# Row maxima, silu and residual rows kept in PSUM, the first stage's calls reordered, and base units moved ahead of the first gathered rows

## The chip, the cores and the metric

One core of a Trainium2 chip runs the whole kernel. The metric is the device time of one execution in microseconds (us); the number quoted is the median of the runs. Below, PE is TensorE, DVE is VectorE, ACT is ScalarE, POOL is GpSimd and SP is SyncE, which here only issues DMAs.

## The reference: what is computed

Two gated sublayers on x of 4 x 256 x 256 (four sequences b, 1024 tokens in eight tiles of 128):

```
q(t, w): s = sqrt(max|t| / max|w|) per column; t/s and w*s are rounded to int8 steps by row;
         the product of the rounded values times both row scales        # smooth-quantised linear
h   = q(layernorm(x), fside);  a = silu(h[:, :128]) * h[:, 128:]
x   = x + tanh(g_xattn) * q(a, ctx)
n   = layernorm(x)
bids = sigmoid(n @ conf_W.T + conf_b) * wealth;  two best of 8 experts, softmax over the two
expert e: g = n @ base_gate + n @ gate_A[e] @ gate_B[e] / 4;  u likewise with up
          y = silu(g) * u;  out_e = y @ base_down + y @ down_A[e] @ down_B[e] / 4
x   = x + tanh(g_ffn) * sum of the two chosen out_e by their weights
```

## The kernel before, in words

**First stage.** For each b the quantised block runs as a chain of short calls, each a Python function with b as its argument: `stats`, `rstd_of`, `x_norm` (layernorm), `w_T`, `x_T1` (transposes), `w_max`, `x_max`, `quotient`, `roots` (column factors), `factors` (PE spreads them along rows), `smooth` (DVE multiplies and takes row maxima), `scale` (ACT rounds), `q1_T`, `q1T_out`, `row_w`, `w_row`, `products1`, `deq1`, `silu1`, `act_up`; then the same for the second product (`a_T`, `a_max`, `roots2`, `factors2`, `smooth2`, `scale2`, `q2_T`, `q2T_out`, `row_c`, `c_row`, `products2`), and the new residual and its layernorm (`x1_rows`, `rstd2_of`, `x1_norm`, `x2_T`, `x2_hi`, `x2_lo`). `logits(b)` gives the routing scores. Every engine executes its calls in a fixed order written out by hand; semaphores between engines do the rest, so a call that has to wait holds up all that stand behind it on its engine.

**Weights.** The second sublayer works in split precision (each weight as a high and a low part, three matmuls per product: lines 55, 57 and 59). 41 chunks of weights go through a ring `raw` of four buffers: SP loads chunk n (line 379) once the low part of chunk n-4 is made, ACT casts the high part (`split`, line 561), POOL subtracts for the low part (`lo`, line 425). Chunks 0 to 7 are the base weights, 8 to 11 the A factors (CH_A is 12), 12 to 27 the B factors, 28 to 36 the down factors (CH_1 is 37), 37 to 40 base_down.

**Base units.** `unit(u)` on PE makes a quarter of the gate and up base products of token tile u//4 (six matmuls of 448 columns, into bank 0 or 4), `unit_out(u)` on ACT copies it out (line 632) and every second one stores it to memory (`base_products`). There are 32. With PRE = 6 tiles, units 0 to 23 come before the plan and 24 to 31 after the first gathered rows.

**Plan and tiles.** After `logits(3)` DVE picks the two experts, PE ranks the pairs (lines 1459 to 1463), DVE works out their places, PE sorts (line 1471), DVE writes the token list (`tok`, line 1091, semaphore `s_plan`). POOL then gathers the normed rows of the first two tiles (`gather`), PE transposes them (`x_T`, line 1488), and 19 tiles of 128 pairs follow: `project_A`, `expand_B`, silu and product, `h_T` (line 1525), `down_products`, scatter. The first tile computes its base products directly (`base_product`, 24 matmuls in pG and pU); the later ones gather them (`gather_base`). On the first tile POOL also makes the low parts of chunks 37 to 40.

Of the kernel before, what the change touches and what calls it, by code (L numbers as in the profile page):

```python
# [23 lines left out]
ALU = mybir.AluOpType  # L24
# [8 lines left out]
P = 128  # L33
EPS = 1e-6
# [30 lines left out]
def build(nc, x, fside, ctxw, g_xattn, g_ffn, wealth, conf_W, conf_b,  # L65
# [22 lines left out]
    with stack:  # L88
# [38 lines left out]
        with part1:  # L127
# [10 lines left out]
            am1 = s1("am1", [P, NB, 4])  # L138
# [7 lines left out]
            am2 = s1("am2", [P, NB, 4])  # L146
# [135 lines left out]
        s_conf = sem("s_conf")  # L282
# [109 lines left out]
        def _(pool):  # L392
# [68 lines left out]
            lo(4)  # L461
            rstd_of(2)
            lo(1)
            roots(0)
            roots(1)
            lo(1)
            rstd_of(3)
            lo(6)
            roots(2)
            lo(1)  # L470
            roots(3)
            lo(6)
            roots2(0)
            lo(3)
            roots2(1)
            lo(2)
            rstd2_of(0)
            roots2(2)
            lo(3)
            rstd2_of(1)  # L480
            lo(5)
            roots2(3)
            lo(4)
            rstd2_of(2)
            lo(1)
            rstd2_of(3)

# [32 lines left out]
            for n in range(CH_1, NCH):  # L520
                split_lo(n)
# [14 lines left out]
        def _(act):  # L536
# [35 lines left out]
            a.activation(warm[:, :], expo[:, 1:2], ACT.Silu).then_inc(s_warm, 1)  # L572
            act.wait_ge(s_rounder, 2)
# [68 lines left out]
            split(12)  # L642
            scale(0)
            split(1)
            scale(1)
            q1T_out(0)
            split(1)
            q1T_out(1)
            w_row(0)
            split(2)  # L650
            silu1(0)
            w_row(1)
            split(4)
            scale(2)
            silu1(1)
            split(2)
            q1T_out(2)
            scale(3)
            scale2(0)
            w_row(2)  # L660
            q1T_out(3)
            q2T_out(0)
            silu1(2)
            split(1)
            w_row(3)
            c_row(0)
            scale2(1)
            split(2)
            q2T_out(1)
            split(2)  # L670
            c_row(1)
            silu1(3)
            split(2)
            x2_hi(0)
            split(2)
            scale2(2)
            split(2)
            q2T_out(2)
            split(1)
            x2_hi(1)  # L680
            split(1)
            unit_out(0)
            c_row(2)
            split(2)
            unit_out(1)
            unit_out(2)
            scale2(3)
            unit_out(3)
            unit_out(4)
            q2T_out(3)  # L690
            x2_hi(2)
            unit_out(5)
            c_row(3)
            unit_out(6)
            unit_out(7)
            unit_out(8)
            x2_hi(3)
            unit_out(9)
            unit_out(10)
            unit_out(11)  # L700
            a.activation(warm[:, :], expo[:, 1:2], ACT.Sigmoid).then_inc(s_warm, 1)
# [3 lines left out]
            for u in range(13, 20):  # L705
                unit_out(u)
# [3 lines left out]
            for u in range(20, 4 * PRE):  # L710
                unit_out(u)
# [66 lines left out]
            for t in range(PRE, NT):  # L778
                base_out(t)
# [27 lines left out]
        def _(dve):  # L807
# [53 lines left out]
            def smooth(b):  # L861
# [11 lines left out]
                link(v.tensor_scalar(sc1[:, b, :], am1[:, b, :], EPS, 1.0 / QMAX, ALU.max, ALU.mult))  # L873
# [29 lines left out]
            def smooth2(b):  # L903
# [5 lines left out]
                link(v.tensor_reduce(am2[:, b, :], q2[:, b], AX_X, ALU.max, apply_absolute_value=True))  # L909
                link(v.tensor_scalar(sc2[:, b, :], am2[:, b, :], EPS, 1.0 / QMAX, ALU.max, ALU.mult))  # L910
                v.reciprocal(inv2[:, b, :], sc2[:, b, :]).then_inc(s_inv2, 1)

            def x1_rows(b):

                dve.wait_ge(s_mm2, b + 1)
                dve.wait_ge(s_a, NB - 1)
                dve.wait_ge(s_crow, b + 1)
                for j in range(TB):
                    ins = v.scalar_tensor_tensor(out=hq[:, 0, j, :], in0=A[b][:, j * H:(j + 1) * H],
# [3 lines left out]
                xv_ = xs_all[:, 2 * b:2 * b + 2, :]  # L923
# [716 lines left out]
```

## Time and profile before

| | |
|---|---|
| median of 3 runs (lowest to highest) | 334.29 us (334.28 to 334.85) |
| the profiled execution, whole | 334.16 us |
| its span, first to last instruction | 332.40 us |
| PE busy / DVE / ACT / POOL | 264.7 / 201.7 / 159.1 / 128.0 us |
| mean granted TensorE clock | 0.90 of full |
| moved by DMA | 45.69 MB, 137 GB/s over the span |

Times inside the span are counted from its start. A row of a timeline gives start, duration, engine, line, operation, output and inputs with shapes and how many instructions it merges; in brackets stands how long the engine was idle before it and what ended that. PE durations overlap, so PE's cost is read from start to start.

### The profile page before, as it was taken

The page shows a single profiled execution, that of the slowest core. Times are in us where ns is not written, and L with a number is a line of the kernel's source. Part 1 is how long each engine was busy: PE and PEld are TensorE (multiplying, and loading weights), DVE is VectorE, ACT ScalarE, POOL GpSimd, SP SyncE. Part 2 cuts the span into 40 slices and gives each one's busy share as a digit, 9 for nine tenths or more (in the row PEclk, how much of TensorE's full clock was granted, in tenths as well). Part 3 has the DMA queues.
Part 4 walks back from the last instruction along what each step waited for, and adds up shares of the span by engine and source line. Part 5 has one row for each costly group of instructions (what it writes and reads, how often), then busy time and mean ns, then how long its engine had stood idle before and what let it go on. Part 6 is the DMA issues. An engine that isn't in the chain of part 4 may idle for free.

```text
span 332.4 us, 5189 instructions
## 1 busy us (share of the span) xinstructions
PE 264.7 (80%) x1556; PEld 241.5 (73%) x1557; DVE 201.7 (61%) x407; ACT 159.1 (48%) x283; POOL 128.0 (39%) x149
## 2 busy tenths in 40 slices
PE   0743947478998959949999999999999999997700
PEld 0532835377986849849999999999999999996600
DVE  1579697968316800166776767676767776775125
ACT  0634979575534413434555555555555555554011
POOL 4489782988000020092333333333333333311111
PEclk9977769659999969987999999999999999999855
DMA  6846351487434422261444444443343444400065
GB/s 192 245 134 169 96 166 55 115 202 236 159 145 166 164 91 110 110 221 34 142 144 134 139 140 142 142 142 134 135 142 142 142 142 142 142 16 18 16 218 176
DMA packets 31342, 45.69 MB, mean 137 GB/s; under 512 B 14104, under 2 KB 25760, under 8 KB 31328
## 3 DMA queue, kind: packets, MB, share of 16 engines
q0 software_dynamic: 4416, 21.50, 19.3%
q1 hardware_dynamic: 20752, 14.03, 14.7%
q10 hardware_dynamic: 6160, 9.98, 8.2%
q8 instruction: 8, 0.13, 0.2%
q14 instruction: 6, 0.05, 0.0%
HBM read 33.57 MB, written 11.93 MB: 137 GB/s over the span
## 4 chain that ended last, share of the span: by engine, by line
PE 64%; DVE 11%; DMA 9%; ACT 6%; POOL 5%; issue 3%; ACTq 1%; SPq 1%; DVEq 0%; POOLq 0%
PE pY L55 8%; PE pY L59 8%; PE pY L57 8%; PE pT L1525 5%; PE pG L55 3%; DMA q<-in_fside_BxS2xS_dram 3%; PE bank L55 3%; PE bank L57 3%; PE bank L59 3%; PE pG L57 3%; PE pG L59 3%; PE pU L57 3%; PE pU L55 3%; PE pU L59 3%; DMA yr<-results 2%
## 5 line engine op out<-in xcount | busy, mean ns | idle before, releaser
L507 POOL DMA_INDIRECT results<-yb,dest x19 | 18.8, 988 | 93.5 <-DVE yb L1173 93.5
L55 PE MATMUL pY<-Wd_hi,hT_hi 128*128 128x384 f32 x133 | 48.3, 363 | 1.0 <-ACT Wd_lo L743 0.8
L59 PE MATMUL pY<-Wd_hi,hT_lo 128*128 128x384 f32 x133 | 45.2, 340 | 0.0
L57 PE MATMUL pY<-Wd_lo,hT_hi 128*128 128x384 f32 x133 | 45.2, 340 | 0.0
L493 POOL DMA_INDIRECT xin<-normed,tok x19 | 18.6, 981 | 38.3 <-DVE share L1093 25.1
L501 POOL DMA_INDIRECT bin<-base_products,tok x18 | 22.0, 1220 | 27.6 <-PE pU L59 17.8
L632 ACT COPY brow<-bank 128x448 f32<-128x448 f32 x32 | 17.0, 532 | 25.6 <-PE bank L59 25.4
L753 ACT CAST hT_hi<-pT 128x896 fp32r<-128x896 f32 x19 | 17.2, 908 | 24.1 <-PE pT L1525 24.1
L729 ACT CAST xaT_hi<-pX 128x256 fp32r<-128x256 f32 x19 | 7.1, 374 | 42.4 <-PE pX L1502 42.0
L55 PEld LDWEIGHTS pY<-Wd_hi,hT_hi 128*128 128x128 f32 x133 | 25.5, 192 | 2.3 <-DVE hT_lo L1161 1.5
L55 PE MATMUL bank<-Wbase_hi,x2T_hi 128*128 128x448 f32 x64 | 25.7, 401 | 0.5 <-ACT brow L632 0.5
L57 PEld LDWEIGHTS pY<-Wd_lo,hT_hi 128*128 128x128 f32 x133 | 25.6, 193 | 0.0
L59 PEld LDWEIGHTS pY<-Wd_hi,hT_lo 128*128 128x128 f32 x133 | 25.4, 191 | 0.0
L57 PE MATMUL bank<-Wbase_lo,x2T_hi 128*128 128x448 f32 x64 | 24.6, 384 | 0.0
L59 PE MATMUL bank<-Wbase_hi,x2T_lo 128*128 128x448 f32 x64 | 24.5, 382 | 0.0
L1157 DVE TENSOR_TENSOR hbuf<-hbuf,gb 128x896 f32<-128x896 f32 x19 | 22.6, 1191 | 1.9
L1161 DVE TENSOR_TENSOR hT_lo<-pT,hT_hi 128x896 fp32r<-128x896 f32 x19 | 20.6, 1082 | 2.8 <-ACT hT_hi L753 2.8
L1130 DVE TENSOR_TENSOR xaT_lo<-pX,xaT_hi 128x256 fp32r<-128x256 f32 x19 | 8.1, 424 | 22.7 <-ACT xaT_hi L729 22.7
L1525 PE MATMUL pT<-ident,hbuf 128*128 128x128 f32 x133 | 18.4, 280 | 4.2 <-DVE hbuf L1157 4.2
L1167 DVE TENSOR_TENSOR zT_lo<-pX,zT_hi 128x128 fp32r<-128x128 f32 x19 | 5.5, 292 | 26.1 <-ACT zT_hi L760 26.1
L747 ACT ACTIVATE gb<-gb 128x896 f32<-128x896 f32 x19 | 18.1, 955 | 5.6 <-DVE gb L1144 5.4
L425 POOL TENSOR_TENSOR WB_lo<-raw,WB_hi 128x448 fp32r<-128x448 f32 x16 | 18.5, 1177 | 5.2 <-ACT WB_hi L561 5.2
(235 smaller groups left out, 739.5 us busy)
## 6 DMA issues: line engine op xcount, KB each, us to landing
base_products<-brow ACTq DMA_DIRECT2D x16, 448.0 KB, 2.5
yr<-results SPq DMA_DIRECT2D x8, 256.0 KB, 4.7
raw<-in_L_ffn_gate_B_dram SPq DMA_DIRECT2D x8, 224.0 KB, 2.6
raw<-in_L_ffn_up_B_dram SPq DMA_DIRECT2D x8, 224.0 KB, 2.6
raw<-in_L_ffn_down_A_dram SPq DMA_DIRECT2D x7, 256.0 KB, 3.0
x_resid<-in_x_dram SPq DMA_DIRECT2D x4, 256.0 KB, 5.2
q<-in_fside_BxS2xS_dram ACTq DMA_DIRECT2D x4, 256.0 KB, 8.0
normed<-q ACTq DMA_DIRECT2D x4, 256.0 KB, 2.7
```

What stands on the lines that cost most here:

```text
L55: m.matmul(outs[i], hi, whi[i], start=first, stop=False, skip_group_check=True)
L57: m.matmul(outs[i], hi, wlo[i], start=False, stop=False, skip_group_check=True)
L59: ins = m.matmul(outs[i], lo, whi[i], start=False, stop=last, skip_group_check=True)
L425: g.tensor_tensor(lo, src, hi, ALU.subtract).then_inc(s_wlo, 1)
L493: g.indirect_dma_start(out=xin[:, :], out_offset=None, in_=xn, in_offset=bass.IndirectOffsetOnAxis(ap=tok[:, j:j + 1], axis=0)).then_inc(d ...
L501: g.indirect_dma_start(out=bin_[:, j % 2].rearrange("p a i -> p (a i)"), out_offset=None, in_=gun, in_offset=bass.IndirectOffsetOnAxis(ap= ...
L507: g.indirect_dma_start(out=yg, out_offset=bass.IndirectOffsetOnAxis(ap=dest[:, j:j + 1], axis=0), in_=yb[:, :], in_offset=None).then_inc(d ...
L747: a.activation(gb[:, :], gb[:, :], ACT.Silu).then_inc(s_silu, 1)
L753: a.copy(hT_hi[:, :, :].rearrange("p c q -> p (c q)"), pT[:, :, :].rearrange("p a q -> p (a q)")[:, 0:I]).then_inc(s_hhi, 1)
L1157: v.tensor_tensor(hbuf[:, :], hbuf[:, :], gb[:, :], ALU.mult).then_inc(s_h, 1)
L1161: v.tensor_tensor(hT_lo[:, :, :].rearrange("p c q -> p (c q)"), pT[:, :, :].rearrange("p a q -> p (a q)")[:, 0:I], hT_hi[:, :, :].rearrang ...
L1525: ins = m.transpose(pT[:, c // 4, (c % 4) * P:(c % 4 + 1) * P], hbuf[:, c * P:(c + 1) * P], ident[:, :])
```

## The change

Row maxima: `smooth` and `smooth2` write them into the first four columns of bank A[b], whose factors have been used by then (both `smooth` multiplies are awaited first), in place of `am1` and `am2` in SBUF. `silu1` writes into bank A[4 + b] and `act_up` reads it there. `x1_rows` makes the new residual in bank A[b]; `bn_stats` and `x1_norm` read it there, and a new ACT call `resid(b)` copies it to `x_resid`; units (bank 0) and logits (bank 1) wait for that copy. SP waits for all of x before the first weight chunk; ACT issues its loads of conf_W, ctx, conf_b and wealth after its two table loads. The sigmoid's table is loaded right after `silu1(3)`. Units up to 29 come before the first gathered rows, 30 and 31 after them, and the direct base products of up and gate stand on either side of `xa_T(0)`. The low parts of chunks 37 to 40 move from POOL to DVE (`late_lo`, semaphore `s_wlo2`).

```diff
 sync:
+            for b in range(NB):
+                sp.wait_ge(d_x[b], 16)
-                    sp.wait_ge(s_wlo, n - RING + 1)
+                    sp.wait_ge(s_wlo, min(n - RING + 1, CH_1))
 gpsimd, after gather_base(2):
-            for n in range(CH_1, NCH):
-                split_lo(n)
 scalar:
-                a.activation(hq[:, b % 2, :, 0:I2], hq[:, b % 2, :, 0:I2], ACT.Silu).then_inc(s_sg, 1)
+                a.activation(A[4 + b][:, 0:2 * I2].rearrange("p (j q) -> p j q", j=TB), hq[:, b % 2, :, 0:I2], ACT.Silu).then_inc(s_sg, 1)
+            def resid(b):
+                act.wait_ge(s_x2, TB * (b + 1))
+                a.copy(xs_all[:, TB * b:TB * (b + 1), :].rearrange("p t h -> p (t h)"), A[b][:, :]).then_inc(s_resid, 1)
...
             x_hi(0)
-            for t in range(PRE, NT):
-                base_out(t)
+            unit_out(4 * NT - 2)
+            unit_out(4 * NT - 1)
 vector, smooth:
-                    dve.wait_ge(s_smooth, 2 * b + w + 1)
-                    v.tensor_reduce(am1[:, b, 2 * w:2 * w + 2], q1[:, b, 2 * w:2 * w + 2, :], AX_X, ALU.max,
+                    dve.wait_ge(s_smooth, 2 * b + 2)
+                    v.tensor_reduce(A[b][:, 2 * w:2 * w + 2], q1[:, b, 2 * w:2 * w + 2, :], AX_X, ALU.max,
 x1_rows:
-                dve.wait_ge(s_a, NB - 1)
-                    ins = v.scalar_tensor_tensor(out=hq[:, 0, j, :], in0=A[b][:, j * H:(j + 1) * H],
+                    ins = v.scalar_tensor_tensor(out=A[b][:, j * H:(j + 1) * H], in0=A[b][:, j * H:(j + 1) * H],
-                xv_ = xs_all[:, 2 * b:2 * b + 2, :]
-                v.tensor_tensor(xv_, xv_, hq[:, 0], ALU.add).then_inc(s_x1, 1)
+                xv_ = A[b][:, :].rearrange("p (t h) -> p t h", t=TB)
+                v.tensor_tensor(xv_, xv_, xs_all[:, 2 * b:2 * b + 2, :], ALU.add).then_inc(s_x1, 1)
...
+            def late_lo(n):
+                _, hi, lo, width = chunks[n]
+                dve.wait_ge(s_whi, n + 1)
+                v.tensor_tensor(lo, raw[:, n % RING, 0:width].rearrange("p (c h) -> p c h", h=H), hi, ALU.subtract).then_inc(s_wlo2, 1)
+            dve.wait_ge(s_resid, NB)
             x_lo(0)
...
             u_add(0, 0, True)
+            late_lo(CH_1)
+            late_lo(CH_1 + 1)
             xa_lo(1)
             h_mul(0)
+            late_lo(CH_1 + 2)
+            late_lo(CH_1 + 3)
 tensor:
-                pe.wait_ge(s_deq2, max(b + 1, 2))
+                pe.wait_ge(s_resid, 2)
...
             x_T(0)
-            base(PRE)
+            unit(4 * NT - 2)
+            unit(4 * NT - 1)
             pe.wait_ge(s_wlo, CH_A)
             project_A(0, group(0))
-            base(PRE + 1)
+            for c in range(HC):
+                base_product(1, c, xT_hi[:, c, :], xT_lo[:, c, :], False)
             xa_T(0)
             pe.wait_ge(s_copied, 4 * NT)
-            for gu in range(2):
-                for c in range(HC):
-                    ins = base_product(gu, c, xT_hi[:, c, :], xT_lo[:, c, :], False)
+            for c in range(HC):
+                ins = base_product(0, c, xT_hi[:, c, :], xT_lo[:, c, :], False)
```

The new orders of the calls, of POOL, ACT, DVE and PE (s, l, u, o stand for `split`, `lo`, `unit`, `unit_out`; 3s is three of them):

```
POOL rstd_of 0 1 2, 2l, rstd_of 3, l, roots 0 1 2, 7l, roots 3, 2l, roots2 0, 2l, roots2 1, l, roots2 2, 3l,
     rstd2_of 0, 2l, rstd2_of 1, l, roots2 3, 2l, rstd2_of 2, 8l, rstd2_of 3, 6l
ACT  8s, scale 0, 2s, scale 1, q1T_out 0, scale 2, w_row 0, q1T_out 1, silu1 0, s, q1T_out 2, w_row 1, s, scale 3,
     silu1 1, w_row 2, 2s, silu1 2, q1T_out 3, s, scale2 0, w_row 3, s, q2T_out 0, 2s, c_row 0, scale2 1, scale2 2,
     q2T_out 1, s, q2T_out 2, c_row 1, silu1 3, sigmoid table, s, resid 0, x2_hi 0, 2s, c_row 2, 2s, o0, s, o1, s, o2,
     s, o3, scale2 3, o4, resid 1, o5, x2_hi 1, q2T_out 3, x2_hi 2, resid 2, o6, 2s, c_row 3, 4s, o7, s, o8, s, o9,
     resid 3, o10, x2_hi 3, s, o11, s, o12, sigmoid, o13 to o20, shares, o21 to o29
DVE  stats 0 1 2, x_norm 0, w_max 0, x_norm 1, w_max 1, x_norm 2, x_max 0, w_max 2, stats 3, x_max 1, c_max 0, w_max 3,
     quotient 0 1, cW_out, x_max 2, quotient 2, c_max 1, x_norm 3, smooth 0 1 2, x_max 3, quotient 3, c_max 2 3, deq1 0,
     smooth 3, act_up 0, deq1 1, a_max 0, act_up 1, deq1 2, smooth2 0, a_max 1, act_up 2, a_max 2, smooth2 1 2,
     x1_rows 0, deq1 3, x1_norm 0, x1_rows 1, act_up 3, x2_lo 0, a_max 3, x1_rows 2, smooth2 3, x1_norm 1 2, x2_lo 1 2,
     x1_rows 3, x1_norm 3, x2_lo 3
PE   ... factors 0 1 2, x_T1 3, q1_T 0 1, row_w 0, products1 0, factors 3, q1_T 2, row_w 1, products1 1, row_w 2,
     products1 2, a_T 0, q1_T 3, factors2 0, a_T 1, row_w 3, products1 3, a_T 2, factors2 1, q2_T 0, factors2 2, row_c 0,
     products2 0, q2_T 1 2, row_c 1, products2 1, row_c 2, products2 2, x2_T 0, a_T 3, u0, u1, factors2 3, u2 to u4,
     x2_T 1 2, u5, q2_T 3, logits 0, u6, logits 1, row_c 3, products2 3, logits 2, u7 to u10, x2_T 3, u11, u12, logits 3,
     u13 to u17, rank, u18 to u23, sort, u24 to u29
```

## Rows read from the trace of the kernel before

**Rows 1.** Busy time by stretch: stretch, length, busy us per engine, clock, DMA

```profile
60.00:73.50 13.50, 7.61 (x36) 6.83 (x37) 11.03 (x21) 7.69 (x17) 12.30 (x13) 0.54 0.70 169
97.10:116.10 19.00, 17.39 (x124) 15.21 (x125) 12.28 (x53) 7.94 (x17) 0.00 (x0) 1.00 0.36 145
121.10:134.90 13.80, 13.40 (x59) 11.98 (x59) 0.85 (x2) 4.64 (x9) 0.96 (x1) 0.82 0.29 111
147.80:303.10 155.30, 155.13 (x959) 146.79 (x960) 107.43 (x174) 79.67 (x123) 53.90 (x51) 0.98 0.37 124
```

**Rows 2.** Timeline of PE between unit 0 and the first tile

```profile
73.52 0.72 PE L55 MATMUL bank<-Wbase_hi,x2T_hi 128*128 128x448 f32 x1
...
97.07 0.45 PE L55 MATMUL bank<-Wbase_hi,x2T_hi 128*128 128x448 f32 x1
...
105.36 0.20 PE L1459 MATMUL bank<-pickb,beforeb 128*128 128x64 bf16 x1 [1.15 <-DVE pickb L1035]
...
106.18 0.45 PE L55 MATMUL bank<-Wbase_hi,x2T_hi 128*128 128x448 f32 x1
...
113.65 0.74 PE L1471 MATMUL bank<-attrib,atrow 128*128 128x76 bf16 x16
...
121.07 0.66 PE L1488 MATMUL pX<-ident,xin 128*128 128x128 f32 x2 [4.13 <-DMA xin<-normed,tok]
...
128.46 0.28 PE L55 MATMUL pX<-WA_hi,xT_hi 128*128 x1
...
139.84 0.38 PE L1488 MATMUL pX<-ident,xin 128*128 128x128 f32 x2
...
147.79 1.75 PE L1525 MATMUL pT<-ident,hbuf 128*128 128x128 f32 x7 [4.16 <-DVE hbuf L1157]
```

**Rows 3.** Timeline of ACT: first rounding, and the sigmoid's table load

```profile
31.52 2.08 ACT L578 ACTIVATE q<-q,rounder,inv 128x256 f32<-128x256 f32 x4
...
99.51 1.28 ACT L701 ACT_TABLE_LOAD   x1 [0.39 <-ACT brow L632]
```

**Rows 4.** The chain that ended last: start, duration, what

```profile
27.68 3.30 DMA raw<-in_L_ffn_up_A_dram
...
117.15 3.78 DMA xin<-normed,tok
```

**Rows 5.** Timeline of DVE in the first stage and the plan

```profile
24.66 1.29 DVE L867 TENSOR_TENSOR q<-q,bank 128x512 f32<-128x512 f32 x2 [1.23 <-PE bank L1268]
...
39.16 0.88 DVE L882 SCALAR_TENSOR_TENSOR hq<-bank,sc,rowb 128x256 f32<-128x256 f32 x2 [2.25 <-ACT rowb L593]
...
53.47 0.88 DVE L882 SCALAR_TENSOR_TENSOR hq<-bank,sc,rowb 128x256 f32<-128x256 f32 x2 [0.72 <-ACT rowb L593]
...
76.54 0.88 DVE L919 SCALAR_TENSOR_TENSOR hq<-bank,sc,rowb 128x256 f32<-128x256 f32 x2 [0.91 <-ACT rowb L599]
...
88.25 0.88 DVE L919 SCALAR_TENSOR_TENSOR hq<-bank,sc,rowb 128x256 f32<-128x256 f32 x2 [0.83 <-ACT rowb L599]
...
101.61 0.23 DVE L1021 TENSOR_TENSOR bids<-bids,rows 128x64 f32<-128x64 f32 x1 [4.14 <-ACT bids L704]
...
115.92 0.18 DVE L1091 TENSOR_SCALAR tok<-dest 128x19 int32<-128x19 int32 x1
```

**Rows 6.** Tile hbuf: ns min/median/max, first to last start

```profile
L1157 DVE TENSOR_TENSOR hbuf<-hbuf,gb x19: 1092/1093/2949, 144.8 to 301.1; 128x896 f32<-128x896 f32 x19
```

**Rows 7.** Groups of ACT up to 140 us, by form

```profile
L621 ACT CAST x2T_hi<-bank 128x512 fp32r<-128x512 f32 x4 | 2.3, 583 | 1.3 <-PE bank L1338 1.0 <-issue 0.3
```

**Rows 8.** Groups of POOL up to 150 us, by form: busy us, mean ns, idle before

```profile
L425 POOL TENSOR_TENSOR WB_lo<-raw,WB_hi 128x448 fp32r<-128x448 f32 x16 | 18.5, 1177 | 5.2 <-ACT WB_hi L561 5.2
```

**Rows 9.** Groups of DVE up to 100 us, by form

```profile
L937 DVE TENSOR_SCALAR q<-x_resid,mv,rstd 128x256 f32<-128x256 f32 x8 | 5.0, 660 | 1.2 <-POOL rstd L457 1.1
...
L888 DVE TENSOR_TENSOR q<-hq 128x256 f32<-128x256 f32 x4 | 3.5, 874 | 0.0
...
L846 DVE TENSOR_SCALAR q<-x_resid,mv,rstd 128x256 f32<-128x256 f32 x8 | 2.9, 405 | 0.0
```

More of the change, by code:

```diff
@@ L465, in _ @@
             roots(1)
-            lo(1)
[L467 to L477, printed above, removed]
+            roots(2)
+            lo(7)
+            roots(3)
+            lo(2)
+            roots2(0)
+            lo(2)
+            roots2(1)
+            lo(1)
             roots2(2)
             lo(3)
+            rstd2_of(0)
+            lo(2)
             rstd2_of(1)
-            lo(5)
+            lo(1)
             roots2(3)
-            lo(4)
+            lo(2)
             rstd2_of(2)
-            lo(1)
+            lo(8)
             rstd2_of(3)
+            lo(6)
             def gather(j):
@@ L640, in base_out @@
                     unit_out(u)
-            split(12)
+            split(8)
             scale(0)
-            split(1)
+            split(2)
             scale(1)
             q1T_out(0)
+            scale(2)
+            w_row(0)
+            q1T_out(1)
+            silu1(0)
             split(1)
-            q1T_out(1)
-            w_row(0)
-            split(2)
[L651 to L655, printed above, removed]
-            split(2)
@@ L657, in _ @@
[L657 to L665, printed above, removed]
+            q1T_out(2)
+            w_row(1)
+            split(1)
+            scale(3)
+            silu1(1)
+            w_row(2)
+            split(2)
+            silu1(2)
+            q1T_out(3)
+            split(1)
+            scale2(0)
+            w_row(3)
+            split(1)
+            q2T_out(0)
@@ L666, in _ @@
+            split(2)
             c_row(0)
             scale2(1)
-            split(2)
+            scale2(2)
             q2T_out(1)
-            split(2)
+            split(1)
+            q2T_out(2)
             c_row(1)
             silu1(3)
-            split(2)
+            a.activation(warm[:, :], expo[:, 1:2], ACT.Sigmoid).then_inc(s_warm, 1)
+            split(1)
+            resid(0)
             x2_hi(0)
             split(2)
-            scale2(2)
-            split(2)
-            q2T_out(2)
@@ L679, in _ @@
[L679 to L682, printed above, removed]
             c_row(2)
             split(2)
+            unit_out(0)
+            split(1)
             unit_out(1)
+            split(1)
             unit_out(2)
+            split(1)
+            unit_out(3)
             scale2(3)
-            unit_out(3)
             unit_out(4)
+            resid(1)
+            unit_out(5)
+            x2_hi(1)
             q2T_out(3)
             x2_hi(2)
-            unit_out(5)
+            resid(2)
@@ L693, in _ @@
+            unit_out(6)
+            split(2)
             c_row(3)
-            unit_out(6)
+            split(4)
             unit_out(7)
+            split(1)
             unit_out(8)
+            split(1)
+            unit_out(9)
+            resid(3)
+            unit_out(10)
             x2_hi(3)
-            unit_out(9)
-            unit_out(10)
+            split(1)
             unit_out(11)
-            a.activation(warm[:, :], expo[:, 1:2], ACT.Sigmoid).then_inc(s_warm, 1)
+            split(1)
@@ L704, in _ @@
             a.activation(bids[:, :, :], bids[:, :, :], ACT.Sigmoid).then_inc(s_sig, 1)
-            for u in range(13, 20):
+            for u in range(13, 21):
                 unit_out(u)
@@ L709, in _ @@
             a.activation(share[:, 1, :], dif[:, :], ACT.Sigmoid, scale=-1.0).then_inc(s_share, 1)
-            for u in range(20, 4 * PRE):
+            for u in range(21, 30):
                 unit_out(u)
@@ L982, in _ @@
             a_max(0)
-            smooth(3)
+            act_up(1)
+            deq1(2)
             smooth2(0)
-            act_up(1)
             a_max(1)
-            deq1(2)
+            act_up(2)
+            a_max(2)
             smooth2(1)
-            act_up(2)
+            smooth2(2)
             x1_rows(0)
-            a_max(2)
             deq1(3)
@@ L1445, in _ @@
             unit(8)
-            x2_T(3)
             unit(9)
             unit(10)
+            x2_T(3)
+            unit(11)
+            unit(12)
             logits(3)
-            for u in range(11, 16):
+            for u in range(13, 18):
                 unit(u)
@@ L1464, in _ @@
             ins.then_inc(s_rank, 1)
-            for u in range(16, 22):
+            for u in range(18, 24):
                 unit(u)
@@ L1473, in _ @@
             ins.then_inc(s_sorted, 1)
-            for u in range(22, 4 * PRE):
+            for u in range(24, 4 * NT - 2):
                 unit(u)
```

121 lines of the change are left out of this document (61 added, 60 removed).

## The prediction

> **What bounds the kernel now.** I read first the busy times by stretch, then the timelines of PE, DVE and ACT up to the first tile, then the chain of waits. From 147.8 to 303.1 us PE is busy for 155.13 of 155.30 us [rows 1]; the change touches nothing in these tiles or behind them, so whatever happens must happen before the first `h_T` at 147.79 [rows 2], and what is won there shifts the rest as a block. That front has four parts. (a) Up to the end of `logits(3)` at 97.07, where unit 11 starts [rows 2], a chain through DVE, ACT and POOL. Its visible fault is order: ACT starts its first rounding at 31.52 [rows 3], half a microsecond after a weight chunk that took 3.30 us has landed [rows 4], though the DVE had finished the first `smooth` about four microseconds earlier (it starts at 24.66, with two multiplies of 1.29 together and two reductions like them [rows 5]). In 60 to 73.5 us PE does 7.61 us of work at a clock of 0.54 [rows 1]. (b) From 97.07 to the rank matmul at 105.36 [rows 2]: the DVE idles 4.14 us until ACT has the sigmoid [rows 5], and ACT spends 1.28 of them on a table load [rows 3]. (c) Rank 105.36, sort 113.65, first gathered rows transposed at 121.07, with PE idle for 4.13 us before it [rows 2]. (d) From 121.07 to 147.79: eight units, the direct base products, the first expansion.
>
> **Part (d), the surest term.** Six units run from 106.18 to 113.65 [rows 2], so a unit costs 1.24 us at full clock. Before, units 24 to 27, which follow `x_T(0)` and begin at the lower clock (1.2 GHz for the first two) after the idle 4.13 us, push `project_A(0)` to 128.46, 7.39 us behind 121.07; then come four units, a wait for the copy and 24 direct matmuls, and the next `x_T` stands at 139.84 [rows 2]: 18.77 us in all; the stretch shows 13.40 of 13.80 us busy at a clock of 0.82 [rows 1]. After: `x_T(0)` 0.3, two units 2.5, `project_A` 0.7, twelve direct matmuls 2.5, `xa_T` 0.25, twelve more 2.5, together 8.7 at full clock, if PE comes there without a pause. The second gathered tile (issued after `x_T(0)`, 3.78 us landing after about 1 us [rows 4]) and `xa_hi`, `xa_lo` lie beside the direct matmuls. Gain 10.1. Cost if that cover is gone: from about 9 us behind `x_T(0)` on, every microsecond by which the second tile or `xa_lo` is later is one at the end.
>
> From 139.84 to 147.79 [rows 2] the path is expansion, `g_add`, `u_add`, `h_mul`. The product took 2.95 us there against a median of 1.09 [rows 6], beside POOL's subtractions. After, POOL only gathers, but DVE has two `late_lo` in front of `h_mul` (128 x 512, 0.65 each by the multiply of [rows 5]). Queued behind these on DVE are `xa_lo(1)` and the product, for which PE's `h_T(0)` waits. 1.86 less, 1.3 to 1.5 more: gain 0.4. The other two `late_lo` lie beside `h_T` and `h_hi`; ACT's casts that they wait for start right after `x_hi(1)`, 3 us earlier than needed. PE idles about 4 us before `h_T(0)` as before, so the slow 1.75 us there and the lower clock after it stay.
>
> **Part (c).** Between rank and sort stand six units in either order, and the DVE's work runs beside: unchanged, 8.29. From the sort to `x_T(0)` before: 7.42, set by plan (115.92 [rows 5]), gather issue and a landing of 3.78 from 117.15 [rows 4]. After, six units (7.45) and the sort's 0.6 stand there: 8.0, so PE is last by a little and has no pause. Loss 0.6, paid for the six units that part (d) no longer has.
>
> **Part (b).** The table is loaded early, so the sigmoid follows the logits in some 0.7 us, and the picks, which let the rank start 3.75 us after 101.61 [rows 2, 5], would let it start about 4.5 us after the logits. But five units (13 to 17, 6.2 us) stand before the rank on PE: 6.2 against 8.29, gain 2.1. Next late there is PE.
>
> **Part (a), laid out call by call** from the new order with the durations of the old trace: `split` 0.5, rounding of four rows 2.08 [rows 3], a full-bank copy on ACT 0.58 [rows 7], a low part on POOL 1.18 [rows 8], chunk load 2.7 to 3.3 [rows 4], `smooth` 2.9, `deq1` 0.88 [rows 5]. Four anchors:
>
> - SP's chunk loads now wait for x, so x and fside share the queues alone and land some 3 us earlier; ACT issues ctx later (from about 10 to 13.5 us) and starts its casts at about 15 instead of 13.4. POOL does `roots(0)` at about 20; `smooth(0)` starts at 23, before 24.66 [rows 5].
> - ACT needs only eight casts before `scale(0)`. The eighth chunk's load waits for POOL's fourth low part, behind `roots(2)`: 23.0 + 1.1 + 2.8 + 0.5 = 27.4, before 31.52. Then two roundings, two casts, `q1T_out(0)` and `scale(2)` put `w_row(0)` at 36 and `deq1(0)` at 36.1, before 39.16 [rows 5].
> - `scale(2)` no longer stands behind six more casts: `deq1(2)` at 43, before 53.47; `x1_rows(2)` at 61, before 76.54 [rows 5].
> - Here the order gives back: ACT now holds one cast between most copies and meets chunks that have not landed (24, 25, 31, 32 and 33 in my layout), and PE has units between. `x1_rows(3)` comes at 76.5, before 88.25 [rows 5]; `rstd2_of(3)` waits behind POOL's eight low parts until 80.6; `x2_hi(3)` ends at 86.5, and `logits(3)`, behind unit 12, at 88.9.
>
> Against 97.07: gain 8.2. The four `resid` copies cost ACT 2.3 us [rows 7]; the one for b = 0 is on the way to unit 0, which waits for it (at 60 us instead of 73.52 [rows 2]), the others stand between units. Units and logits wait for `resid(0)` and `resid(1)`, about 1 us after the norm that they need anyway; the DVE's wait for the last `resid` before `x_lo(0)` is over by 26 us.
>
> **Values in PSUM.** The trace has no DVE or ACT write into PSUM. Nearest rows: the same `act_up` with both inputs in SBUF takes 0.87 in the mean, beside POOL [rows 9]; `deq1` from a bank takes 0.44 for 256 columns [rows 5]. I take the durations from banks without POOL's share; `x1_norm`, 0.66 in the mean from SBUF and 0.41 for the same form in `x_norm` [rows 9], goes to 0.42. Bounds: a gain of 1.5 us more on the path (no residue of POOL's anywhere) and a loss of 2 (a write to a bank as slow as the worst read beside POOL).
> A rule speaks against this part. The Trainium skill, VectorE: DVE Perf Modes, section "Why PSUM operands drop a tier", says that an operand in PSUM takes a single-source fp32 operation out of its double-rate mode. By it the eight `x1_norm` would take about 0.8 each, an estimate, and lose 3.3 us of DVE time. The trace disagrees so far: `x_norm`'s 0.405 us for 256 columns from SBUF [rows 9] is no faster than 0.44 from a bank [rows 5].
>
> **Sum.** 8.2 + 2.1 - 0.6 + 10.1 + 0.4 = 20.2 off the first `h_T`. Hand-overs that I set at almost nothing, and more traffic in 10 to 20 us, I price at 1.0 back: 19.2. Span 332.40 - 19.2 = 313.2; the profiled execution lasts 334.16, 1.76 more than its span, so 315.0. The median of the runs, 334.29, is 0.13 above that execution, which I leave aside. Own range of this case 311 to 319.
>
> **The rivals.**
> 1. The first stage doesn't move (chunks hold up ACT's calls as much as before, only at other places). For it: PE, ACT and POOL are coupled through four buffers, and the layout has few spare microseconds at the end. Against: `scale(2)` and `deq1(2)` have ten microseconds. Then only (b) to (d) count, 12.0 less the 1.0: 323.
> 2. The units run without a pause from 60 us on. From unit 0 to `x_T(0)` PE has 30 units (37.2) and about 10 us of transposes, logits, rank and sort, 47 against the 51 that I laid out: 4.3 less, about 310.5. For it: DVE and POOL have slack there. Against: the unlanded chunks.
> 3. Slower: ACT's casts, now one between copies, meet unlanded chunks far oftener. Place: ACT between `c_row(2)` and `x2_hi(3)`, where each such cast holds up the copy that frees a bank, and with it the units and POOL's next low part, on which the next load waits. Price up to 3.3 us each [rows 4]. I count five; six more give the gain back, and eight more give 315 + 26 = 341.
> 4. PE still pauses before `x_T(0)` because the gathered rows come late (three stores of base products run beside this gather, one before), and the next matmuls run at the lower clock: 1 to 2 us of wait and up to 2 us of slow units, 319.
> 5. Bank operands at half rate, the rule above: `x1_norm(3)`, `x1_norm(1)` and the bank writes on the path together about 1.7, 316.7.
>
> **How the numbers follow.** Forecast 315.0: 0.60. Rival 1 0.15, rival 2 0.09, rival 3 0.04, rival 4 0.07, rival 5 0.03; 0.02 that gains and losses cancel. The range 308.5 to 323 takes in the forecast, rivals 2, 4, 5 and half of rival 1. A measurement of this kernel can tell some 0.2%: faster 0.94, same 0.02, slower 0.04.
>
> **What would show it.** First `scale` of ACT near 27, `deq1(2)` near 43, `logits(3)` ending near 89, rank near 95, plan near 106, no idle row of PE before `x_T(0)` near 111.5, 8.7 us from there to the next `x_T`, first `h_T` near 128, and the same 155 us of tiles after it. The prediction is wrong if ACT shows waits for chunk loads of more than some 10 us between 60 and 90, or if the time of the tiles changes.

## The result, and the profile after

| | before | after |
|---|---|---|
| median of four runs each (lowest to highest) | 334.57 us (334.28 to 334.85) | 312.19 us (311.93 to 313.76) |
| ratio of after to before, 95% interval | | 0.9341 [0.9308, 0.9374] |
| the profiled execution, whole / span | 334.16 / 332.40 us | 311.93 / 310.20 us |

The forecast was 315.0, with a range of 308.5 to 323. The direction and the size are right; the sum is made of terms that did not all come as written. Every ratio, here and below, is against the kernel before, measured together with that variant; its median was 335.4 to 336.3 us beside the experiments, so times from different experiments are compared by their ratios. A median counts all runs, while a ratio leaves out those more than 1.5% above the fastest of the same kernel.

The timeline of PE of the changed kernel, with the marks that answer [rows 2] (start, duration, engine, line, operation, count, in brackets the idle time before it and what ended it):

```profile
59.14 0.71 PE L55 MATMUL bank<-Wbase_hi,x2T_hi 128*128 128x448 f32 x1 [0.46 <-issue]
...
82.51 0.48 PE L55 MATMUL bank<-Wbase_hi,x2T_hi 128*128 128x448 f32 x1 [2.28 <-ACT brow L634]
...
83.53 0.58 PE L55 MATMUL bank<-Wbase_hi,x2T_hi 128*128 128x448 f32 x1
...
90.75 0.45 PE L55 MATMUL bank<-Wbase_hi,x2T_hi 128*128 128x448 f32 x1
...
96.96 0.20 PE L1485 MATMUL bank<-pickb,beforeb 128*128 128x64 bf16 x1
...
105.19 0.73 PE L1497 MATMUL bank<-attrib,atrow 128*128 128x76 bf16 x16
...
113.20 0.38 PE L1514 MATMUL pX<-ident,xin 128*128 128x128 f32 x2
...
115.88 0.28 PE L55 MATMUL pX<-WA_hi,xT_hi 128*128 x1
...
121.70 0.38 PE L1514 MATMUL pX<-ident,xin 128*128 128x128 f32 x2
...
128.99 0.98 PE L1551 MATMUL pT<-ident,hbuf 128*128 128x128 f32 x7 [3.50 <-DVE hbuf L1168]
```

In order: unit 0, unit 9 and its second high-part matmul, the end of `logits(3)` (taken below, too, as the start of the unit behind it, here unit 13), rank, sort, `x_T(0)`, `project_A(0)`, `x_T(1)`, the first `h_T`. The idle time before `x_T(0)` is gone, and rank and sort find their operands ready. Taken between these marks, the gain of 22.2 us of span lies here:

| part | before | after | gain | forecast |
|---|---|---|---|---|
| (a) start to the end of `logits(3)` | 97.07 | 90.75 | 6.3 | 8.2 |
| (b) to the rank | 8.29 | 6.21 | 2.1 | 2.1 |
| (c) rank to sort, sort to `x_T(0)` | 8.29, 7.42 | 8.23, 8.01 | -0.5 | -0.6 |
| (d) `x_T(0)` to `x_T(1)` | 18.77 | 8.50 | 10.3 | 10.1 |
| (d) `x_T(1)` to the first `h_T` | 7.95 | 7.29 | 0.7 | 0.4 |
| hand-overs | | | (in the rows) | -1.0 |
| first `h_T` to the second | 10.58 | 8.34 | 2.2 | 0 |
| second to last `h_T` | 144.62 | 144.82 | -0.2 | 0 |
| last `h_T` to the end | 29.41 | 28.05 | 1.4 | 0 |

Up to the first `h_T` the gain is 18.8 against 19.2 forecast, by terms that miss in both directions; 3.4 more lie behind it, where PE executes the same matmuls. Busy time by stretch, as [rows 1] (length, busy us of PE, PEld, DVE, ACT, POOL with counts, clock, DMA share, GB/s):

```profile
60.00:73.50 13.50, 11.99 (x66) 10.73 (x65) 5.80 (x16) 7.66 (x17) 8.89 (x10) 0.91 0.76 225
90.75:110.00 19.25, 19.25 (x137) 17.48 (x137) 12.42 (x53) 7.67 (x17) 2.02 (x2) 1.00 0.48 184
128.99:281.50 152.51, 152.37 (x955) 143.84 (x956) 108.34 (x176) 79.59 (x123) 52.41 (x49) 1.00 0.38 128
```

In 60 to 73.5 us PE now works 11.99 us at a clock of 0.91, where it had 7.61 at 0.54 [rows 1]; from the end of `logits(3)` to 110 us it never pauses, and the tiles fill PE as before. The first stage on DVE, as [rows 5] (`smooth(0)`, `deq1(0)`, `deq1(2)`, `x1_rows(2)`, `x1_rows(3)`, `x1_norm(3)`):

```profile
21.87 1.28 DVE L879 TENSOR_TENSOR q<-q,bank 128x512 f32<-128x512 f32 x2 [1.63 <-PE bank L1290]
...
34.12 0.88 DVE L894 SCALAR_TENSOR_TENSOR hq<-bank,sc,rowb 128x256 f32<-128x256 f32 x2 [0.98 <-ACT rowb L591]
...
41.32 0.88 DVE L894 SCALAR_TENSOR_TENSOR hq<-bank,sc,rowb 128x256 f32<-128x256 f32 x2
...
59.62 0.88 DVE L930 SCALAR_TENSOR_TENSOR bank<-bank,sc,rowb 128x256 f32<-128x256 f32 x2
...
76.73 0.88 DVE L930 SCALAR_TENSOR_TENSOR bank<-bank,sc,rowb 128x256 f32<-128x256 f32 x2 [1.55 <-ACT rowb L597]
...
81.78 1.00 DVE L948 TENSOR_SCALAR q<-bank,mv,rstd 128x256 f32<-128x256 f32 x2 [2.36 <-POOL rstd L457]
```

and on ACT, as [rows 3] (`scale(0)`; then casts that wait for their chunk, and `x2_hi(3)`):

```profile
25.53 2.07 ACT L576 ACTIVATE q<-q,rounder,inv 128x256 f32<-128x256 f32 x4
...
80.00 0.62 ACT L554 CAST WdA_hi<-raw 128x512 fp32r<-128x512 f32 x1 [2.33 <-DMA raw<-in_L_ffn_down_A_dram]
81.41 0.62 ACT L554 CAST WdA_hi<-raw 128x512 fp32r<-128x512 f32 x1 [0.79 <-DMA raw<-in_L_ffn_down_A_dram]
...
87.66 0.59 ACT L623 CAST x2T_hi<-bank 128x512 fp32r<-128x512 f32 x1 [0.32 <-issue]
```

The anchors were 23, 36.1, 43, 61, 76.5 and, for `scale(0)`, 27.4. The first four came one to two microseconds earlier than laid out. The fifth was hit, so the stretch from the fourth to the fifth was 1.6 us longer than laid out. From there the stage lost 1.9 us: two casts wait 2.33 and 0.79 us for their chunks, the copy behind them frees unit 9's bank late, PE pauses for 2.28 us, units 9 and 10 run mostly at the lower level (1.2 GHz; granted clock 0.58 from 82.51 to 86.61; 0.58 us a matmul against 0.37; 4.10 us for the two, where two units at full clock take 2.5), and `x2_hi(3)` ends at 88.25 instead of 86.5.

### The profile page after: what moved, and what is told of

The parts are those of the page before. It is cut to its first block, busy times and chain, and to the rows that moved or that the text cites. A ratio compares the mean times of both kernels' runs of the same rounds, so it can differ in the third digit from the quotient of the medians.

```text
span 310.2 us, 5194 instructions
## 1 busy us (share of the span) xinstructions
PE 257.4 (83%) x1556; PEld 236.0 (76%) x1557; DVE 195.1 (63%) x411; ACT 160.3 (52%) x287; POOL 121.4 (39%) x145
## 4 chain that ended last, share of the span: by engine, by line
PE 69%; DMA 9%; ACT 8%; POOL 5%; DVE 4%; issue 2%; SPq 1%; ACTq 1%; DVEq 0%
PE pY L55 9%; PE pY L59 8%; PE pY L57 8%; PE pT L1551 5%; PE bank L55 3%; PE bank L57 3%; PE bank L59 3%; PE pG L55 3%; PE pU L57 3%; PE pG L59 3%; PE pG L57 3%; PE pU L59 3%; PE pU L55 3%; PE bank L1290 2%; DMA x_resid<-in_x_dram 2%
## 5 line engine op out<-in xcount | busy, mean ns | idle before, releaser
L55 PE MATMUL pY<-Wd_hi,hT_hi 128*128 128x384 f32 x133 | 47.6, 358 | 1.0 <-ACT Wd_lo L755 0.8
L1168 DVE TENSOR_TENSOR hbuf<-hbuf,gb 128x896 f32<-128x896 f32 x19 | 20.8, 1092 | 1.9
L1551 PE MATMUL pT<-ident,hbuf 128*128 128x128 f32 x133 | 17.7, 273 | 3.5 <-DVE hbuf L1168 3.5
```

The costliest lines, as they stand in the source:

```text
L55: m.matmul(outs[i], hi, whi[i], start=first, stop=False, skip_group_check=True)
L1168: v.tensor_tensor(hbuf[:, :], hbuf[:, :], gb[:, :], ALU.mult).then_inc(s_h, 1)
L1551: ins = m.transpose(pT[:, c // 4, (c % 4) * P:(c % 4 + 1) * P], hbuf[:, c * P:(c + 1) * P], ident[:, :])
```

## Experiments

### Which part of the change carries the gain

**units_only**: the kernel before with the moved units alone.

```diff
-            for u in range(22, 4 * PRE):
+            for u in range(22, 4 * NT - 2):
...
             x_T(0)
-            base(PRE)
+            unit(4 * NT - 2)
+            unit(4 * NT - 1)
...
-            base(PRE + 1)
+            for c in range(HC):
+                base_product(1, c, xT_hi[:, c, :], xT_lo[:, c, :], False)
             xa_T(0)
```

> The kernel before with one part alone: units 24 to 29 ahead of the first gathered rows, direct products split around xa_T(0). Theory (the parts add up): logits(3) ends at 97 and rank and sort stay at 105.4 and 113.7; eight units instead of two follow the sort, so the first x_T comes about 3 us later (124), and 8.5 instead of 18.8 us lie between it and the next x_T: 7 us less, 327, and up to 4 less still if the clock then holds at the first tile: 323 to 327. Rival (the units are the whole change, the first stage only moves waits): 314 or less.

Measured: 327.08 us, ratio 0.9736 [0.9676, 0.9797]. Sort, `x_T(0)` and `x_T(1)` on PE:

```profile
114.83 0.74 PE L1471 MATMUL bank<-attrib,atrow 128*128 128x76 bf16 x16
...
125.33 0.38 PE L1488 MATMUL pX<-ident,xin 128*128 128x128 f32 x2
...
133.85 0.38 PE L1488 MATMUL pX<-ident,xin 128*128 128x128 f32 x2
```

From `x_T(0)` to `x_T(1)` it takes 8.52 us, where [rows 2] have 18.77: the 10.1 of part (d) is there without the rest. Some 3 us go back ahead of it: eight units instead of two now stand between the sort and `x_T(0)`, 10.50 us for 7.42.

**stage1_only**: the changed kernel with the units put back.

```diff
-            for u in range(24, 4 * NT - 2):
-                unit(u)
...
             x_T(0)
-            unit(4 * NT - 2)
-            unit(4 * NT - 1)
+            base(PRE)
```

> The changed kernel with the units put back: 24 before the first gathered rows, 8 and both direct products behind. Theory: logits(3) ends at 90.7, rank at 97, sort at 105.2 as in the changed kernel, PE idles about 4 us before the first x_T at 112.6, then 18.8 us: 324 to 327. Rival (the order of the first stage is worth nothing without the units): 332 or more.

Measured: 321.17 us, ratio 0.9584 [0.9521, 0.9646], 3 us less than expected: `logits(3)` ends at 88.28, 2.5 earlier than in the profile of the changed kernel. The rank stands at 94.50, the sort at 102.73. PE then waits for the gathered rows:

```profile
88.28 0.45 PE L55 MATMUL bank<-Wbase_hi,x2T_hi 128*128 128x448 f32 x1
...
109.39 0.66 PE L1512 MATMUL pX<-ident,xin 128*128 128x128 f32 x2 [5.93 <-DMA xin<-normed,tok]
```

The rows come 6.66 us behind the sort here, and a gather takes 2.7 to 3.0 us to land. In the changed kernel it takes 3.5 to 3.7; its first gather starts at 108.68, so the rows are there 0.8 to 1.0 us before PE asks for them at 113.20. Rival 4 looked at the right place, where little is to spare, but its pause did not come. The two halves multiply to 0.9736 x 0.9584 = 0.9331, against 0.9341 for both together: within intervals of some 0.6% each they add up.

**no_psum**: the changed kernel with row maxima, silu and residual in SBUF again, and without the `resid` copies.

```diff
-                    v.tensor_reduce(A[b][:, 2 * w:2 * w + 2], q1[:, b, 2 * w:2 * w + 2, :], AX_X, ALU.max,
+                    v.tensor_reduce(am1[:, b, 2 * w:2 * w + 2], q1[:, b, 2 * w:2 * w + 2, :], AX_X, ALU.max,
...
-                    ins = v.scalar_tensor_tensor(out=A[b][:, j * H:(j + 1) * H], in0=A[b][:, j * H:(j + 1) * H],
+                    ins = v.scalar_tensor_tensor(out=hq[:, 0, j, :], in0=A[b][:, j * H:(j + 1) * H],
```

> The changed kernel with row maxima, silu and new residual rows back in SBUF, without the four copies of the residual; all orders as in the change. Theory (holding values in PSUM is worth only DVE's waits beside POOL): single DVE instructions of the first stage grow to 1 to 2 us again, logits(3) 1 to 3 us later, 313 to 316. Rival (the values in PSUM make the new order pay): logits(3) near 97, 319 or more.

Measured: 313.17 us, ratio 0.9327 [0.9249, 0.9404]; span 310.8 against 310.2. **small_psum**, the kernel before with row maxima and silu in banks (the same lines the other way round, without the residual):

> The kernel before with row maxima and silu in PSUM and nothing else changed. Theory: the DVE instructions of these lines fall to 0.16 and 0.4 us, but ACT, which waits for chunks, sets the pace: 0 to 2 us less, 332.5 to 334.5. Rival: the waits beside POOL were on the path, 4 us or more less, 330 or less.

Measured: 334.85 us, ratio 0.9987 [0.9949, 1.0025]. So the values in PSUM, which the title names first, are worth nothing that can be measured (the intervals are 0.4% to either side in small_psum and 0.8% in no_psum), though they do change the instructions: in small_psum `act_up` takes 396 ns in the mean, where [rows 9] have 874, and `logits(3)` still ends at 97.63. DVE's groups by form up to 100 us, first of the changed kernel, then of no_psum (busy us, mean ns, idle before):

```profile
L948 DVE TENSOR_SCALAR q<-bank,mv,rstd 128x256 f32<-128x256 f32 x8 | 3.9, 535 | 2.7 <-POOL rstd L457 2.7
...
L858 DVE TENSOR_SCALAR q<-x_resid,mv,rstd 128x256 f32<-128x256 f32 x8 | 2.9, 403 | 0.0
```

```profile
L947 DVE TENSOR_SCALAR q<-x_resid,mv,rstd 128x256 f32<-128x256 f32 x8 | 7.9, 1038 | 2.7 <-POOL rstd L459 2.7
...
L856 DVE TENSOR_SCALAR q<-x_resid,mv,rstd 128x256 f32<-128x256 f32 x8 | 2.9, 401 | 0.0
```

In the new order most of `x1_norm` runs beside POOL's low parts. From SBUF it takes 1038 ns in the mean there (401 to 1368) and 401 in `x_norm`, L856; from a bank 535 in the same place (515 to 546). The bank saves DVE 4 us, and the end of `logits(3)` doesn't follow: 89.79 in no_psum, 90.56 and 90.75 in two profiles of the changed kernel. DVE waits 2.7 us for `rstd` there in either case. The Trainium skill, SBUF — State Buffer, section "Who interferes with whom", says that `tensor_scalar` from SBUF can take a port pair that DVE shares with GpSimd and that one of the two then stands still for a whole instruction; 1038 against 401 agrees. The other rule, weighed in the prediction (rival 5: half rate from PSUM, about 0.8), does not show: 535 is a third more than 403, not twice as much, though more than the 0.42 us that the prediction took.

### The smaller moves

**table_late**: the changed kernel with the sigmoid's table load back behind `unit_out(11)`.

> The changed kernel with the sigmoid's table load back at its old place, behind unit_out(11). Theory (the five units ahead of the rank set its time, the picks are ready 1.8 us earlier in the changed kernel): the sigmoid comes about 1.3 us later, the rank still at the end of unit 17: 0 to 0.5 us more, ratio 0.934 to 0.936. Rival (the 4.14 us that DVE idled before was the table): 2 to 4 us more, ratio 0.940 or more.

Measured: 311.66 us, ratio 0.9287 [0.9232, 0.9342]. The load on ACT, and the one pause that it makes on PE before the rank:

```profile
88.05 1.28 ACT L713 ACT_TABLE_LOAD   x1
```

```profile
90.02 0.47 PE L55 MATMUL bank<-Wbase_hi,x2T_hi 128*128 128x448 f32 x1 [0.30 <-ACT brow L634]
```

`logits(3)` ends at 88.26, the sigmoid stands at 89.87, and the rank still finds its operand, but at 6.77 us behind `logits(3)` instead of 6.21: the copy of unit 12 waits behind the load, and unit 14 for that copy. So the earliest place is worth 0.6 us, as expected, and not the 2.1 of part (b). That the table has no share in the 2.1 isn't shown. Five units stand between `logits(3)` and the rank before the change, too (11 to 15), and there PE waited 1.15 us for the picks [rows 2], since the load began 2.4 us behind `logits(3)` [rows 2, 3]. Behind `unit_out(11)` in the new order it begins 0.2 us ahead of it; a load behind `unit_out(13)`, which would be the old place as seen from `logits(3)`, wasn't tried.

**pool_lo**: the changed kernel with the low parts of chunks 37 to 40 back on POOL.

> The changed kernel with the low parts of chunks 37 to 40 back on POOL. Theory (an exchange: two late_lo leave the path, the product waits beside POOL again): the product of the first tile 2.9 us in place of 1.1, PE idle 4.2 in place of 3.5 us, 0.5 to 1 us more, and up to 3 more if the clock falls at the first h_T, ratio 0.935 to 0.945. Rival (POOL's subtractions hold the gather of the third tile, too): 5 us or more.

Measured: 312.86 us, ratio 0.9286 [0.9217, 0.9354]. DVE's product before the first `h_T`, and POOL beside it:

```profile
125.55 2.98 DVE L1170 TENSOR_TENSOR hbuf<-hbuf,gb 128x896 f32<-128x896 f32 x1
```

```profile
123.78 5.33 POOL L425 TENSOR_TENSOR Wd_lo<-raw,Wd_hi 128x512 fp32r<-128x512 f32 x4
```

PE idles 4.19 us before this `h_T`, against 3.50 with the `late_lo`: the move is worth 0.7, where 0.4 was forecast, and is too small to be seen in the time. The ratio expected was 0.935 to 0.945. The four variants measured together (table_late, pool_lo, casts_far and casts_later) have 0.926 to 0.929, all below the 0.934 and 0.935 of the changed kernel measured at other times, so their ratios are held against each other.

**early_dma**: the changed kernel with the load order of before: SP doesn't wait for x, and ACT issues conf_W, ctx, conf_b and wealth before its table loads.

> The changed kernel with its two changes of the load order undone: SP no longer waits for x before the first weight chunk, and ACT issues conf_W, ctx, conf_b and wealth ahead of its two table loads, as before the change. Theory: the load order is worth part of the first stage's 6.3 us. The first smooth falls back from 21.87 to about 24 (24.66 in the kernel before), unit 0 from 59.14 to about 61, the end of logits(3) from 90.75 to about 92.5, and the time is 1 to 2 us above that of the changed kernel in this call. Rival: the chain behind the first smooth has slack by the order of the calls, so unit 0 stays at 59 to 60 and the time within 0.7 us.

Measured: 313.92 us, ratio 0.9353 [0.9276, 0.9431], against 314.00 for the changed kernel measured beside it (again, below). `smooth(0)`:

```profile
21.54 1.28 DVE L877 TENSOR_TENSOR q<-q,bank 128x512 f32<-128x512 f32 x2 [1.63 <-PE bank L1288]
```

That lies between 21.10 and 21.87 of two profiles of the changed kernel; unit 0 starts at 58.26 (58.44 and 59.14). The theory falls: the new load order gains nothing that can be measured. What remains of the changes ahead of `smooth(0)` is the hand-written orders of POOL and DVE (`roots(0)` behind three low parts instead of five); that this alone brings the 3 us was not tried.

### What is late at the end of the first stage

**casts_far**: all casts between `c_row(3)` and `x2_hi(3)` on ACT (there are six; the expectation below says eight) moved behind the latter, and `rstd2_of(3)` on POOL moved ahead of the low parts that depend on them. **casts_later**: two of the six moved, and nothing on POOL.

```diff
 casts_far, ACT:
             c_row(3)
-            split(4)
             unit_out(7)
-            split(1)
             unit_out(8)
-            split(1)
...
 POOL:
-            lo(8)
-            rstd2_of(3)
             lo(6)
+            rstd2_of(3)
+            lo(8)
...
 ACT, behind x2_hi(3), after the copy of each of units 13 to 20:
+                split(1)
```

> The changed kernel with two of the four casts behind c_row(3) moved behind x2_hi(3). Theory (the casts that wait for chunks there hold the copy of unit 7 and so PE): no pause of PE before unit 9, x2_hi(3) bound by rstd2_of(3) at about 84.5, logits(3) ending 2 to 4 us earlier, near 87: 309 to 311, ratio 0.924 to 0.930. Rival (the chain through rstd2_of(3) and x1_norm(3) sets the end anyway): within 0.5 us of the changed kernel.

> The changed kernel with all eight casts between c_row(3) and x2_hi(3) moved behind it, the last of them between units 13 to 19, and rstd2_of(3) behind six low parts in place of eight. Theory: the same pause gone and the norm of b = 3 about 1 to 2 us earlier too, logits(3) near 86.5: 4 us less than the changed kernel, 308 to 310, ratio 0.920 to 0.927. Rival: the late chunks then hold the first tile (the A and B factors of down are needed there), and nothing is won or 1 to 3 us lost.

Measured: casts_later 313.88 us, 0.927 [0.918, 0.936], the ratio as expected and the time 3 us above, and its profile is not read here; casts_far 311.81 us, 0.9263 [0.9199, 0.9326], the ratio as expected and the time 2 us above. In casts_far the pause before unit 9 is gone and `logits(3)` ends at 87.05, 3.7 us earlier than in the changed kernel. It changes two things at once, but of the two it is the casts that held the stage: in the changed kernel `x1_norm(3)`, which waits for `rstd2_of(3)`, is done at 82.8, and the transposes behind it start on PE at 86.61 only, right behind unit 10. But the gain doesn't reach the end: table_late and pool_lo, measured beside it, have 0.9287 and 0.9286. The rank and sort of casts_far, on PE:

```profile
94.08 0.20 PE L1483 MATMUL bank<-pickb,beforeb 128*128 128x64 bf16 x1 [0.70 <-DVE pickb L1044]
...
104.13 0.72 PE L1495 MATMUL bank<-attrib,atrow 128*128 128x76 bf16 x16 [1.63 <-DVE attrib L1082]
```

Now DVE's planning is late, and it is slower than in the changed kernel. Three of its small instructions in casts_far, with POOL beside them, and then the same three in the changed kernel:

```profile
92.99 1.03 DVE L1044 CAST pickb<-gp 128x64 bf16<-128x64 f32 x1
...
94.08 1.21 DVE L1047 CAST fcol<-icol 128x128 f32<-128x128 int32 x1
...
97.97 1.02 DVE L1069 TENSOR_TENSOR place<-place,gp 128x64 f32<-128x64 f32 x1
```

```profile
90.17 5.03 POOL L425 TENSOR_TENSOR WdA_lo<-raw,WdA_hi 128x512 fp32r<-128x512 f32 x4 [2.31 <-ACT WdA_hi L554]
...
96.17 1.29 POOL L425 TENSOR_TENSOR WdB_lo<-raw,WdB_hi 128x512 fp32r<-128x512 f32 x1 [0.97 <-ACT WdB_hi L554]
97.62 1.29 POOL L425 TENSOR_TENSOR WdB_lo<-raw,WdB_hi 128x512 fp32r<-128x512 f32 x1 [0.16 <-ACT WdB_hi L554]
```

```profile
94.97 0.20 DVE L1046 CAST pickb<-gp 128x64 bf16<-128x64 f32 x1
95.20 0.22 DVE L1049 CAST fcol<-icol 128x128 f32<-128x128 int32 x1
...
99.49 0.23 DVE L1071 TENSOR_TENSOR place<-place,gp 128x64 f32<-128x64 f32 x1
```

Beside a low part 0.2 us becomes 1.0 to 1.2, six times in the plan. So casts taken out of the way of the logits put their low parts into the way of the plan: 3.7 us gained at the logits, 1.1 left at the sort (104.13 against 105.19) and at the first `h_T` (127.92 against 128.99). Behind that the clock decides: the second `h_T` stands at 137.26, against 137.33 in the profile above and 138.57 in another of the same kernel (again, below).

### Is the rest the clock?

**again**: the changed kernel once more.

> The changed kernel once more, as the measure for the run beside it and for the clock. Theory: the clock behind the first h_T is not set by the change. From the first h_T to the second there were 8.51 us in the first profile of this kernel, 9.5 to 9.6 in variants that idle for the same 3.50 us before it; a second profile may show any length from 8.5 to 10, and the time of the execution follows it. Likewise the pause of 2.28 us before unit 9 and the lower clock in units 9 and 10 need not return: then logits(3) ends at 88 to 89 instead of 90.75. Rival: both are properties of the code; the second profile shows 8.5 from h_T to h_T and a pause of 2.2 to 2.4 us before unit 9 with logits(3) ending at 90.5 to 91.

Measured: 314.00 us (313.39 to 315.40), ratio 0.9354 [0.9298, 0.9410]; the profiled execution lasts 314.56, its span 312.8. Busy time from the first `h_T` to the second, first in the profile above (the expectation counted 8.51 there, to a mark 0.17 behind the second `h_T`), then in again (columns as in [rows 1]):

```profile
128.99:137.33 8.34, 8.34 (x50) 7.77 (x51) 5.82 (x8) 4.14 (x6) 2.20 (x2) 1.00 0.19 70
```

```profile
128.80:138.57 9.77, 9.77 (x50) 9.10 (x51) 5.92 (x8) 4.14 (x6) 2.20 (x2) 0.83 0.16 58
```

And PE behind the last `h_T`, in the same two:

```profile
286.09 0.41 PE L55 MATMUL pY<-Wd_hi,hT_hi 128*128 128x384 f32 x1 [0.82 <-ACT Wd_lo L755]
286.69 0.34 PE L55 MATMUL pY<-Wd_hi,hT_hi 128*128 128x384 f32 x1
```

```profile
287.25 0.66 PE L55 MATMUL pY<-Wd_hi,hT_hi 128*128 128x384 f32 x1 [0.82 <-ACT Wd_lo L755]
288.35 0.52 PE L55 MATMUL pY<-Wd_hi,hT_hi 128*128 128x384 f32 x1
```

The same code, with the same idle time before these matmuls (3.50 at the first `h_T`; 1.47 or 1.46, then 0.82 at the last), runs once at full clock and once partly at the lower level. The difference is 1.43 us at the first place and 1.43 at the second (29.48 us from the last `h_T` to the end against 28.05). Across the variants the first `h_T` after the same 3.50 us takes 0.98, 1.46, 1.62, 1.75 or 1.76, and in small_psum it was quick after a longer idle time, with the lower level only behind it:

```profile
147.34 0.99 PE L1525 MATMUL pT<-ident,hbuf 128*128 128x128 f32 x7 [4.18 <-DVE hbuf L1157]
```

At the end the old order has 29.41 us in one kernel (before), 30.4 in a second (units_only) and 28.2 in a third (small_psum), so the 1.4 there is not a matter of the code. The new one has 28.0 to 28.5 in seven profiles and 29.48 in again; whether the change makes the lower level rarer at the end isn't shown. Between the first two `h_T`, 1.43 of the 2.2 us is chance. The old order there took 10.0 to 10.7 us in three profiles and the new one 9.3 to 9.8 in six beside the 8.34; pool_lo, with the low parts where they were, took 9.48. PE is busy all the time in nearly all of them, and the granted clock is 0.74 in the 10.58 us of before, 0.83 in the 9.77 of again and 1.00 in the 8.34: the length goes with the clock. Up to 0.8 may still belong to the change, and that is not settled. The second half of the theory fell. Unit 9 in again:

```profile
83.63 0.47 PE L55 MATMUL bank<-Wbase_hi,x2T_hi 128*128 128x448 f32 x1 [0.83 <-ACT brow L634]
```

The pause before it shrank, but `logits(3)` ended at 90.56 all the same, since unit 7 and half of unit 8 ran at the lower level this time. ACT's wait for the chunk is the same in both (2.39 against 2.33); only its price on PE changes its form.

## Why the prediction was right, and where it was not

- **(d), 10.1, and its cover.** Right to 0.2. PE comes to `project_A(0)` without a pause (113.20 to 115.88), and the direct matmuls hide the second gathered tile. units_only shows the same 8.5 us alone. The second part of (d) gained 0.7 for 0.4.
- **(b), 2.1, and (c), -0.6.** Right to 0.1, and PE is next late at both places, as said. How much of (b) the early table load gives is open: its place is worth 0.6 us against table_late, and its old place as seen from `logits(3)` wasn't tried.
- **(a), 8.2.** Measured 6.3: the term that was mis-sized. The anchors held up to `x1_rows(3)` (76.73 against 76.5). The step that failed is the last one, "`x2_hi(3)` ends at 86.5, and `logits(3)`, behind unit 12, at 88.9": the layout had chunks that have not landed there and their waits, but not that the pause on PE is followed by units at the lower level, which is some 1.6 of the 1.9 us that it is late. stage1_only, with the same code up to there, ended `logits(3)` at 88.28 and table_late at 88.26, below the 88.9; the two profiles of the changed kernel at 90.56 and 90.75, the other variants with these casts between. So the order gives 6.3 to 8.8 us, as the chunks land and the clock falls, and 8.2 lies inside that.
- **"SP's chunk loads now wait for x ... land some 3 us earlier".** Wrong as a cause: early_dma has the same `smooth(0)` without it.
- **Hand-overs, -1.0.** No such loss shows between the marks; it stood in for part of what (a) lost.
- **"so the slow 1.75 us there and the lower clock after it stay".** Wrong as a rule. The idle time stayed (3.50 for 4.16), the lower clock came in six of the seven profiles with the new order there, for differently long, and not in the first one of the changed kernel. The 1.43 us there are luck of that execution, and the 1.4 behind the last `h_T` are the lower level in the profile of before, which small_psum, with the same code there, doesn't show. Together that is 2.8 of the 3.4 us, and it brought the profiled execution 3.1 us below the forecast; that of again, 314.56, stands 0.4 below it. By its own second sign, the time of the tiles, the prediction holds between the second and the last `h_T` (144.62 and 144.82), and not at the two ends.
- **Rivals.** 1 (the stage doesn't move) and 3 (unlanded chunks oftener): the casts of chunks wait 8.1 us in seven waits between 58 and 92 us, below the limit of ten that was set and little more than the 7.2 of the kernel before, and stage1_only shows the stage moving. 2 (units without a pause): only casts_far comes near, and there the plan takes it back. 4 and 5: above.

Left open: which of the new orders (POOL, ACT or DVE) gives how much of the 6.3 to 8.8 us of (a); they depend on each other and were only tried together. A ring of more than four chunk buffers, which might take the waits out at their root, wasn't tried.

## What to carry to other kernels

Independent matmuls belong where PE would wait for a chain on other engines: moving six units from behind the gathered rows to ahead of them brought ten microseconds behind these rows, as counted from start to start, and seven net where the rest of the order was the old one. Where engines run hand-written orders, lay out the new order call by call with the durations of the old trace; here it held to two microseconds up to 77 us, and where casts met late chunks and the clock could fall, a range of 2.5 us was due. A place for a value (PSUM or SBUF) that makes an instruction faster is worth nothing while its engine waits for another: here DVE saved 4 us and the time stayed.

## What the runs showed of the hardware

- The lower clock after a pause is not a property of the code: with 3.50 us idle before the first `h_T` the matmuls behind it ran at a granted clock of 1.00 in one profile and of 0.83 in another of the same kernel, a difference of 1.4 us there and as much again at the end. The Trainium skill, TensorE: Matmul & The Clock Gate, section "What's actually happening", says that the gate's watch runs free of the kernel, so that the point of change varies; the two profiles agree. A difference of 1 to 3 us behind a pause needs a second profile before it is put down to an edit.
- DVE instructions of 0.2 us took 1.0 to 1.2 us beside POOL's subtractions of 1.26 us (casts_far, in the plan), casts and two-input operations alike.
